# First attention: the relative scores of a unit are made five units ahead of their use instead of four

## The reference, cut to what matters

```python
dist = jnp.clip(idx[None, :] - idx[:, None], -R, R) + R          # R = 64
pe_k, pe_v = rel_emb_k[dist], rel_emb_v[dist]
score = einsum('bhqd,bhkd->bhqk', q, k) + einsum('bhqd,qkd->bhqk', q, pe_k)
attn = softmax(score)
ctx = einsum('bhqk,bhkd->bhqd', attn, v) + einsum('bhqk,qkd->bhqd', attn, pe_v)
x = x + ctx @ W_out + b_out + ffn0(xn)
```

## Time and profile before

| | |
|---|---|
| median of 3 runs | 2499.93 us (2491.85 to 2500.97) |
| the profiled execution's own time | 2499.09 us |
| its span in the profile | 2497.3 us |
| busy share of the span: PE, DVE, ACT, POOL | 88%, 77%, 69%, 34% |
| units 0 to 255 in the trace | about 443.6 to 1554.2 us |

### The profile page before, as it was taken

One profiled execution on the slowest core, in us unless ns is written; L12 is line 12 of the kernel. 1 busy time (PEld: TensorE's weight loads), 2 busy tenths in 40 slices (PEclk: granted clock), 3 DMA queues, 4 the chain that ended last, 5 costly groups with the idle time before them and its releaser, 6 DMA issues. The chain is left out here.

```text
span 2497.3 us, 91017 instructions
## 1 busy us (share of the span) xinstructions
PE 2200.2 (88%) x34464; PEld 1779.8 (71%) x34464; DVE 1921.7 (77%) x7669; ACT 1711.4 (69%) x5582; POOL 842.6 (34%) x911
## 2 busy tenths in 40 slices
PE   6999998788888888888888888979999699999998
PEld 5888887577777777777677777657877466666665
DVE  6787772567877777777777777758888598898888
ACT  2333332677777777777677777966666599999998
POOL 3666665020222211122122212321212556566562
PEclk9999999799999999999999999989999799999999
DMA  7867552666676667676666666013231111111110
GB/s 237 238 164 192 115 119 43 160 161 159 170 174 161 167 166 168 168 171 169 166 171 169 168 167 154 23 66 119 95 111 69 47 27 42 30 36 38 27 39 14
DMA packets 360774, 304.80 MB, mean 122 GB/s; under 512 B 25368, under 2 KB 328856, under 8 KB 358952
## 3 DMA queue, kind: packets, MB, share of 16 engines
q1 hardware_dynamic: 349864, 271.93, 43.2%
q0 software_dynamic: 10496, 27.28, 3.7%
HBM read 166.43 MB, written 132.69 MB: 120 GB/s over the span
## 5 line engine op out<-in xcount | busy, mean ns | idle before, releaser
L819 ACT ACTIVATE probs<-neg_scores,low 128x256 f32<-128x256 f32 (+1 forms) x1152 | 574.0, 500 | 227.2 <-DVE low L955 210.6
L955 DVE CUSTOM_DVE_ANT_0 neg_scores<-scores,rel_bias 128x256 f32<-128x256 f32 x1024 | 373.4, 421 | 231.3 <-PE scores L1124 110.2
L1114 PE MATMUL scores<-k_heads,q_heads 32*128 32x256 f32 (+1 forms) x2304 | 208.4, 426 | 162.7 <-DVE rel_s L963 136.3
L1136 PE MATMUL probsT<-consts,probs 128*128 128x128 f32 x2240 | 315.9, 284 | 5.1 <-issue 4.7
L1687 DVE CUSTOM_DVE_ANT_0 neg_scores<-scores,alibi 128x128 f32<-128x128 f32 (+1 forms) x896 | 265.9, 353 | 57.4 <-PE scores L1743 54.0
L771 POOL TENSOR_SCALAR q_heads<-q_raw,consts,q_bias 128x256 f32<-128x256 f32 x128 | 69.4, 557 | 614.2 <-ACT q_raw L802 614.1
L1136 PEld LDWEIGHTS probsT<-consts,probs 128*128 128x128 f32 x2240 | 245.7, 143 | 37.6 <-issue 10.6
L1114 PEld LDWEIGHTS scores<-k_heads,q_heads 32*128 32x128 f32 x2304 | 99.4, 186 | 225.8 <-DVE low L955 154.1
L274 POOL TENSOR_TENSOR hid<-hid,gate_bc 128x512 f32<-128x512 f32 x160 | 205.3, 1288 | 151.6 <-DVE hid L445 144.2
L300 ACT ACTIVATE ga<-gate_up 128x512 f32<-128x512 f32 x160 | 95.6, 598 | 223.3 <-PE gate_up L511 221.6
L963 DVE COPY rel_s<-scores 128x768 f32<-128x768 f32 x256 | 244.0, 953 | 4.2 <-PE scores L1124 2.8
(11 more groups left out here) (204 smaller groups left out, 4983.3 us busy)
## 6 DMA issues: line engine op xcount, KB each, us to landing
rel_rows<-rel_s SPq DMA_DIRECT2D x256, 192.0 KB
rel_bias<-rel_rows SPq DMA_DIRECT2D x256, 192.0 KB, 3.6
gate_bc<-gate_rows SPq DMA_DIRECT2D x32, 1024.0 KB, 10.7
rel_rows<-rel_s SPq DMA_DIRECT2D x256, 128.0 KB
rel_bias<-rel_rows SPq DMA_DIRECT2D x256, 128.0 KB, 3.6
packed<-ffn_in SPq DMA_DIRECT2D x8, 1280.0 KB, 15.7
xe<-packed SPq DMA_DIRECT2D x16, 640.0 KB, 3.9
expert_out<-ye POOLq DMA_DIRECT2D x16, 640.0 KB, 3.2
```

Source lines behind the costliest of these rows:

```text
L819: act.activation(probs[s % 3][:, j, 0:w], neg[s % 2][:, j, 0:w], ACT.Exp, bias=low[s % 3][:, j:j + 1], scale=-1.0, accum_out=sums[s // UB ...
L955: dve.tensor_tensor_reduce(neg[s % 2][:, j, 0:w], S_ps[:, 512 * j:512 * j + w], bias_of(s)[:, j, :] if s < NU0 else alibi[:, 4 * j + s % 4 ...
L1114: ins = pe.matmul(S_ps[:, 512 * j:512 * j + w], q_of[b % 2][rows, i, qt * P:(qt + 1) * P], k_of[b % 2][rows, 0:w], start=True, stop=True)
L1136: ins = pe.transpose(PT_ps[kt][:, j * P:(j + 1) * P], probs[u % 3][:, j, kt * P:(kt + 1) * P], ident)
```

## The change

`LEAD` goes from 4 to 5. Nothing else is edited.

```diff
@@ -550,7 +550,7 @@
             NU0 = UB * nb
             NB0 = nb + LATE
             NUL = UB * NB0
-            LEAD = 4
+            LEAD = 5
```

## The result

The changed kernel takes 2397.81 us (median of 4 runs, 2395.31 to 2401.78) against 2498.02 us before (4 runs): ratio 0.9599, 95% interval 0.9584 to 0.9615.

A forecast was written before the change was run, and what follows sets the result against it. The prediction took a loop of waits with late bias reads as the bound: 2499.1 - 96.6 + 7 + 12 + 1 = 2422.5, so 2423 us (chance 0.83). Range 2399 to 2451, or 2460 with the near half of rival A.

The forecast's parts named there:

- The bound and the mechanism: First attention: a loop of waits; the two-step chain of copy, write, issue and landing takes 7.8 to 8.8 us.
- Lateness: VectorE's first additions: 134 of 256 units start late for their bias; all late starts go, -96.6 us.
- Not passed: TensorE's gaps ahead of the scores: the smaller of lateness and gap, step by step, lets 90 of 97.8 us pass; +7.
- Taken back by uneven steps: Early arrivals in short steps partly stand before long ones: 0.05 us a step, +12 us, ends 0 and +40.
- Clock: Granted clock in the first attention: fewer gaps give back at most 22 us; counted 0, with -15 as an end.
- The start: Ahead of unit 0, one more relative and copy: +1.0 us, between 0 and +2.
- Queries and SP's buffers: Next batch's queries, needed a step earlier, keep over 3 us of cover; SP's bias-buffer wait is already met: 0.
- the haircut: The +12 us taken back for uneven steps in the first attention.
- A: First attention: TensorE's own work is the bound more often than gaps say; gain 38 us, 2461; chance 0.09.
- B: Bias reads are late for bandwidth, so earlier issue lands as late as before: no gain, 2500; chance 0.04.
- C: Next batch's queries come too late for r = 3 and stall TensorE and VectorE: slower, 2564; chance 0.04.
- The rule that the prediction takes from the Trainium skill: Bias transfers: 2.0 us plus bytes over 436 GB/s, 2.45 us per 192 KB half; the change would gain nothing.

The follow-up runs named there:

- held-back reads: Changed kernel (LEAD 5) with every bias read issued one unit later in the queue: 2493.8 us against 2496.4 before the change; on slow chips 1.0022 and 1.0042.
- The three held-back runs: Changed kernel with bias reads one write later for units r = 0, 6, 7, for r = 2, 3, 4, 5, or all: 28.2, 65.4, 93.1 us above it.
- the delay of known length: Changed kernel plus one 0.95 us VectorE copy ahead of the additions of units r = 1 to 4 of each batch: 2524.2 us, 123.5 above it.
- the run without reads: Changed kernel (LEAD 5) with the bias reads and the wait for them left out: 2399.1 us against 2402.9 for the changed kernel.

## Why the prediction was right in kind and wrong in size

**The bound and the mechanism** were right. The two-step chain of copy, write, issue and landing made starts late, five units of lead removed every late start, and undoing the release alone (held-back reads, 0.9994) undid all of it.

**Lateness, -96.6 us**: confirmed. It is gone in the profile after, and brought back it was 101.7 us.

**Not passed, +7**: confirmed in kind. The step-by-step test gave 27.4, 71.6 and 95.4 us for 28.2, 65.4 and 93.1 measured. The 90 of 97.8 us in the prediction also counts units under 0.1 us; less the 4.5 us that the changed kernel shows in such a count, some 85.5 pass and the term is +11.

**Taken back by uneven steps, +12**: this is the step that failed, and it is what put the forecast too high. I wrote that "early arrivals in the short ones will partly stand before the long ones". Measured: 123.5 of 125 us of added delay show. The three held-back runs lie 5 us above, 2 us under and 2 us above the fourth column of the table. With the clock's part in them taken off at 0.33 us (3.4, 0 and 7.9 us) that is 2 above, 2 under and 6 under. So the term is 0 within some 6 us. It double-counted, too. Where a start stood before another bound was already in the +7, and the floor of 3.85 us for a step was busy time that included matmuls at half clock. Its upper end of +40 was not even what I called it: half of what is left between a gain of 89.6 and one of 38.4 us is 26.

**Clock, 0 with -15 as an end**: mis-sized. Together with the late reads 20.5 us at half speed went; at 0.33 us for each, -7 us. That price is from one pair of runs on another chip and applied here, not measured in this kernel. One of the seven pieces followed a gap ahead of a projection, so it is not shown that the late reads brought all of them.

**The start, +1**: right. The chain behind the third copy was as worked out: unit 0 starts 5.1 us behind it in all three profiles of the changed kernel, 4.05 before. The whole attention began at another moment in each of these profiles (third copy at 440.0 to 441.0, 439.5 before), so that unit 0 started 1.5 to 2.5 us later than in the kernel before.

**Queries and SP's buffers, 0**: right. The queries had 3.4 us of cover at the least in the changed kernel, where the prediction left over 3 us. LEAD 6 used that up, and it lost.

With these terms as the prediction counts them: -96.6 + 7 + 0 - 7 + 1 = -96 us; with +11 in place of +7, -92. Measured were 96, 100 and 100 us on three chips. Up to 9 us stay open. The 256 units took 1008.4, 1013.0 and 1008.6 us in the three profiles of the changed kernel, so much of that can be one execution against another.

The low end of the range did not hang on the haircut: it let all 96.6 us show and took nothing back. What it held too small was the clock, 5 us where 7 came by the price above and I had myself named 15. The rest is a matter of luck. The range was worked out from 2499.9 us for the kernel before, which came out at 2498.0 beside the changed one; as a gain the low end is 100.9 us, and 100.2 were measured. So the 1.2 us outside the range say little. The 23 us between the forecast gain and the measured one say more, and half of them are the haircut.

**The rivals**: A (TensorE's own work takes most back) is out by the delay of known length, B by the run without reads, C by the profile, where only the first batch waits for its queries. The rule that the prediction takes from the Trainium skill, page "DMA: Bandwidth & Descriptors", section "Anatomy of one DMA — SWDGE (gpsimd) path", would have left no gain, as B would. The trace stays against it on SyncE's path: the reads landed in 3.0 us at the least and 3.6 at the median after the change too.

## What to carry to other kernels

Count lateness unit by unit against all the other things that a start waits for: the waits view named 75 us of a lateness of 97. Then pass it through the gaps of the engine that follows, once; here nothing more had to be taken off for unevenness, within some 6 us. And before moving a transfer earlier in a queue by its own wait, look at what stands behind it. A read that waits for its own write at the head of an ordered queue turned a hoped-for gain into 245 us of loss, while one more unit of lead gave the whole gain, and two more lost 18 us of it to another chain.

## What the hardware showed that I had not expected

The same kernel took about 2500 us on some chips and 2707 to 2713 us on two others. With held-back reads TensorE was idle for 73 us in the stretch under no named releaser there, and 18.5 us in the same kernel on a good chip; its mean clock was 0.95 instead of 0.98. The cause was not looked for. There six units of lead gained 64 and 74 us, on a good chip 77.

A gap of 4.02 us on TensorE was followed by half clock in the very next matmuls. With the same delay spread over four steps, where TensorE's gaps are about 1 us (176.1 us in 162 places), there was no half clock behind 468 us in the run on the good chip, and 15 pieces on the slow one.
